# Graph network kernel, scatter stage: GpSimd's pause in mid-group waits for three scatters instead of four

## What is computed

```
x_i, x_j = x[dst_or_src of each edge], edge_attr: 64 numbers of each edge
out_i = act(concat(x_i, edge_attr) @ W)            # 4 heads of 64
out_j = act(concat(x_j, edge_attr) @ W)
alpha = act((concat(out_i, out_j) * att).sum(-1))  # one number of each edge and head
alpha = act(batch_norm(alpha))
alpha = segment_softmax(alpha, i)                  # over the edges with the same i = src
x = layernorm(x + segment_sum(out_j * alpha, i).mean(heads) + bias)
h = gcn_conv(gcn_conv(x, src, dst, W1, b1), src, dst, W2, b2)
x = layernorm(x + relu(h))
```

## Time and profile before

| | |
|---|---|
| median of 3 runs | 7369.46 us |
| profiled execution, its own time | 7374.29 us |
| its span in the profile | 7372.1 us |
| from the first scatter of the scatter stage to the last | 534.65 to 3270.51 us |
| scatters in it | 1616, in 202 groups |
| busy share over the whole span | TensorE 69%, VectorE 72%, ScalarE 55%, GpSimd 27% |
| mean granted TensorE clock over the span | 0.861 of full speed |

### The profile page before, as it was taken

How to read it: one execution, slowest core, us unless ns; L and a number is a source line. 1 busy time by engine, 2 the same in 40 slices (tenths; PEclk the granted TensorE clock), 3 DMA queues, 4 the chain that set the end, 5 groups by cost and what they waited for, 6 DMA issues and landing times. The chain is left out here.

```text
span 7372.1 us, 162457 instructions
## 1 busy us (share of the span) xinstructions
PE 5061.6 (69%) x33039; PEld 3158.5 (43%) x33040; DVE 5308.0 (72%) x27929; ACT 4071.5 (55%) x10690; POOL 2017.3 (27%) x2671
## 2 busy tenths in 40 slices
PE   1226766666666766637777777777724999995877
PEld 0113444344344443424444444444413555554877
DVE  5626666666666666629999999999987888887122
ACT  0015555455555555537777777777735889884000
POOL 0035555555655555541111111111100000000000
PEclk8557778778888778869999999999967999997978
DMA  4565555555555555555555555555514878773956
GB/s 33 219 226 166 178 165 177 169 165 178 170 177 168 171 174 164 172 175 144 144 145 145 144 146 144 144 145 145 144 34 121 214 213 222 213 214 103 381 225 258
DMA packets 905819, 1259.82 MB, mean 171 GB/s; under 512 B 267668, under 2 KB 774531, under 8 KB 884180
## 3 DMA queue, kind: packets, MB, share of 16 engines
q1 hardware_dynamic: 783812, 843.53, 41.2%
q0 software_dynamic: 88656, 333.99, 12.1%
q10 hardware_dynamic: 33216, 80.75, 3.2%
HBM read 832.07 MB, written 425.87 MB: 171 GB/s over the span
## 5 line engine op out<-in xcount | busy, mean ns | idle before, releaser
L840 POOL DMA_INDIRECT rows<-rowS,idx x1616 | 1605.0, 993 | 1151.7 <-DMA rows<-rowS,idx 605.1
L1530 DVE CUSTOM_DVE_ANT_1 junk<-bufh,attb 128x128 bf16<-128x128 f32 x7296 | 1693.7, 292 | 3.7 <-ACT bufh L1570 3.7
L1096 PE MATMUL psa<-one_c,one_s 128*128 128x392 bf16 x2352 | 651.4, 395 | 763.7 <-issue 322.7
L2219 PE MATMUL psm<-msg,onem 128*128 128x260 f32 x3648 | 1011.5, 402 | 135.1 <-issue 50.8
L989 ACT ACTIVATE lgS<-preS 128x1024 f32<-128x1024 f32 x404 | 412.7, 1021 | 893.0 <-remote 638.3
L2219 PEld LDWEIGHTS psm<-msg,onem 128*128 128x128 f32 x3648 | 619.1, 189 | 527.0 <-issue 473.0
L1502 POOL COPY eaC<-bufh 128x128 f32<-128x128 f32 x912 | 322.0, 353 | 1793.9 <-DMA bufh<-rows 1789.1
L923 DVE TENSOR_SCALAR one_c<-ioc,code 128x392 bf16<-128x392 f16 x2352 | 779.1, 331 | 18.3 <-DVE code L915 3.7
L1566 ACT ACTIVATE lg<-pre 128x512 f32<-128x512 f32 x912 | 544.9, 598 | 423.4 <-PE pre L1609 423.3
L2186 DVE TENSOR_TENSOR msg<-oj,alpha 128x512 f32<-128x512 f32 x912 | 631.1, 692 | 185.7 <-issue 96.7
L915 DVE TENSOR_SCALAR code<-pairS,codes 128x3 f32<-128x3 f32 x784 | 201.4, 257 | 782.2 <-remote 531.8
(11 more groups left out here) (275 smaller groups left out, 8107.7 us busy)
## 6 DMA issues: line engine op xcount, KB each, us to landing
bufh<-rows SPq DMA_DIRECT2D x912, 322.0 KB, 3.0
oj<-rows SPq DMA_DIRECT2D x912, 256.0 KB
adj<-adj SPq DMA_DIRECT2D x98, 1568.0 KB, 8.4
adj<-cnts ACTq DMA_DIRECT2D x49, 1568.0 KB
eaS<-in_edge_attr_dram SPq DMA_DIRECT2D x201, 256.0 KB
low<-dlow SPq DMA_DIRECT2D x202, 252.0 KB
rows<-fill POOLq DMA_DIRECT2D x20, 1610.0 KB
rows<-fill POOLq DMA_DIRECT2D x100, 322.0 KB
```

The lines of the kernel that those rows point to most:

```text
L840: eng.indirect_dma_start(out=m["rows"][h], out_offset=bass.IndirectOffsetOnAxis(ap=idx[s][:, k:k + 1], axis=0), in_=rows[s][:, k, :], in_o ...
L1096: mm = eng.matmul(psa[r][:, 0:z.GC], one_s[r][:, k, :], one_c[r][:, k, :], start=(k == 0), stop=(k == GT - 1))
L1530: ins = eng.tensor_tensor_reduce(junk[q][:, k * H + h, :, :], buf[j][:, k, :, h * D:(h + 1) * D], attb[:, :, h, :], 1.0, 0.0, ALU.mult, AL ...
L2219: mm = eng.matmul(psm[j][:, 0:C + H], one[q][:, k, :], msg[q][:, k, :], start=(k == 0), stop=(k == UT - 1))
```

## The change

A scatter k with k < FIRST = K // 2 - 1 = 3 now signals a semaphore of its own, `early[s]`. The other five (k = 3 to 7) still signal `sent[s]`. The pause waits for `early[s]`, that is for the scatters k = 0, 1 and 2 of this group, and no longer for k = 3. The three waits for `sent` elsewhere count five scatters in a group instead of eight. The instructions and their order are the same on every engine.

```diff
+    FIRST = K // 2 - 1
...
+        early = [sem(ctx, f"early{s}") for s in range(NR_BUF)]
         sent = [sem(ctx, f"sent{s}") for s in range(NR_BUF)]
...
                         eng.indirect_dma_start(
                             out=m["rows"][h], out_offset=bass.IndirectOffsetOnAxis(ap=idx[s][:, k:k + 1], axis=0),
-                            in_=rows[s][:, k, :], in_offset=None).then_inc(sent[s], 16)
+                            in_=rows[s][:, k, :], in_offset=None).then_inc(early[s] if k < FIRST else sent[s], 16)
                     if part == 0:
-                        eng.wait_ge(sent[s], b * 16 * K + 16 * K // 2)
+                        eng.wait_ge(early[s], (b + 1) * 16 * FIRST)
...
-                eng.wait_ge(sent[s], (NG + NR_BUF - 1 - s) // NR_BUF * 16 * K)
+                eng.wait_ge(sent[s], (NG + NR_BUF - 1 - s) // NR_BUF * 16 * (K - FIRST))
...
-                wait(eng, sent[s], b * 16 * K)
+                wait(eng, sent[s], b * 16 * (K - FIRST))
                 eng.tensor_copy(rows[s][:, :, LO], m["nlo"][:, span(t * K, K)])
...
-                wait(eng, sent[s], b * 16 * K)
+                wait(eng, sent[s], b * 16 * (K - FIRST))
                 eng.wait_ge(ea_in[s % 2], ea_landed(b, s))
```

## The result

The changed kernel takes 7507.5 us, the median of four runs (7499.45 to 7530.64), against 7368.3 us for the kernel before. The ratio is 1.0191, with a 95% interval of 1.0161 to 1.0221. That is 139 us slower, on the side of rival C and outside the predicted range. The profiled execution has a span of 7528.5 us.

The account below looks back on a forecast made before the run. The scatter stage was taken as bound by waits, with GpSimd like a server behind a queue. Gains of 9 us (last groups) and 74 us (the other 195) made 83 us, so 7369.5 - 83 = 7286 us, range 7150 to 7500.

Parts of the forecast that it names:

- rival C: Scatter stage: the shorter pause no longer lets held-up signals through, so engines stay held; 155 us slower, 7525 us; 37%.
- The pause: GpSimd's mid-group idle time falls from 2.4 to 1.1 us, 1.27 us less in each of 202 groups, 257 us at most.
- Rival D: Landings of k = 2 and k = 3 bunch, so the pause stays as long; 7369 us; 18% together with no change.
- The semaphore and the counts at nothing: The new semaphore and wait counts add or move no instruction, so they cost nothing.
- Scatters and VectorE at nothing: Scatters overlapping a little more with VectorE cost 0; doubling today's collision loss would cost 48 us more.
- The comparison with 3.1 us: A skill text gives 3.1 us for a transfer blocked by VectorE; no scatter took over 1.41 us, so the trace disagrees.
- A faster GpSimd lives in this regime: In the first 195 groups GpSimd soon catches up with ScalarE; pace 13.18 us instead of 13.56, 74 us gained.
- The last seven groups: From group 195 on GpSimd alone works off its queue, so each group gains 1.27 us, 9 us in all.
- point of decision: Rival C hangs on a needed quiet time between 0.30 and 1.4 us; at under 1.1 us it is dead.
- One of its signs: Under rival C, remote waits of ScalarE's Exp and VectorE's `code` grow beyond 638 and 532 us, ending at a group's start.
- The reading of the earlier trace: In two groups ScalarE's Exp and VectorE's `code` come loose inside GpSimd's pause, 1.38 to 1.90 us after k = 3.
- Rival A: The whole pause time is gained because the other engines follow GpSimd's rhythm; 257 us, 7112 us; 20% with anything between.

Follow-up runs that it names:

- e1: Changed kernel with FIRST = K // 2, so the pause waits for all four scatters on the new semaphore: 7368.2 us, ratio 0.9993 to the kernel before.
- e3: Changed kernel plus a 1.3 us GpSimd memset behind the early wait, lengthening the time without scatters: 7363.4 us, ratio 0.9992 to the kernel before.
- e4: Changed kernel with the pause moved behind k = 2, still waiting for k = 0, 1 and 2: 7401.1 us, ratio 1.0036 to the kernel before.
- h_after: The changed kernel itself, run again on a chip where the kernel before takes 7517.0 us: 7373.4 us, ratio 0.9805.
- j_first_two: Changed kernel with two scatters on the early semaphore instead of three, pause still behind k = 3; before at 7512.4 us: 6770.6 us, ratio 0.9014.
- f_m20: Kernel before with the mid-group landing wait replaced by a GpSimd memset of about 2.0 us; before at 7511.2 us: 7116.4 us, ratio 0.9472.
- g_no_pause_again: Kernel before with the mid-group landing wait removed and nothing in its place; before at 7514.9 us: 6753.3 us, ratio 0.8988.
- g_tiny: Kernel before with the mid-group landing wait replaced by a GpSimd memset of 8 numbers a partition; before at 7514.9 us: 6755.4 us.

## Why the prediction was wrong

- *The pause.* Right in kind: the landing of k = 2 ends it, under 1.2 us after k = 3 in 82 of 202 groups and 1.27 in the median, about as the earlier trace rows less 1.27 gave (1.1). The landing waits fell to 223 us, further than the 350 forecast. Rival D falls.
- *The semaphore and the counts at nothing.* Right (e1, 0.9993).
- *Scatters and VectorE at nothing.* Right: 985 ns in the mean, 993 before, and none over 1444 ns. The comparison with 3.1 us proves less than it says, since no instruction of VectorE in that stage lasts over 0.63 us, and none could keep a scatter waiting for 3.1 us by itself.
- *"A faster GpSimd lives in this regime … I take 13.18 as the pace with the shorter pause."* This step failed. It priced the changed kernel by a stretch of before, in which each group still had its pause of 2.4 us. The other engines' pace was held constant, while the change touches just what sets it. With the shorter pause the first 195 groups take 2811.9 us, 14.42 each, not 13.18. The term of 74 us gained came as 167 us lost. GpSimd's waits for the Ln went to 472 us, not to about 250. The last seven groups gained 6 us for the 9 forecast.
- *Rival C* named the mechanism, and its size came out close: 14.40 us a group from the earlier trace rows, 155 us slower forecast, 139 measured. That it came so close is partly luck, since it took every group for starved, while 107 of 201 groups began after more than 1 us of idle time (14 before). Its point of decision was right too, since 1.1 us is mostly too short on this chip. One of its signs was wrong: the remote waits of Exp and `code` fell. The held-up time went to earlier waits, the counts and `ranks`. The part on their ends was half right: they left the pause behind k = 3, but only 130 of 393 moved to a group's start.
- *The reading of the earlier trace rows.* For the Exp it holds. For VectorE it doesn't: the row puts `code`'s wait down to a load of the pairs and not to a remote signal, and in the next group `code` starts at 2028.96, when k = 4 has just begun, and again behind such a load. The 531.8 us of remote waits are real but were not looked at.
- *The weights.* The 37% for C rested on two groups and on "may simply be the latency of that event". Counted over the stage, the same trace has 292 of 367 such waits ending in the pauses, which are 24% of it. That is no chance. It could not tell a latency from a needed quiet time, though. That took the runs: a shorter pause loses (7507.5), the same early landings with a longer quiet time don't (e3, 7363.4), and the ends follow the pause when it is moved (e4).
- *Rival A* was not wrong in general. On chips without the hold the change gains 144 us of A's 257, and no pause at all gains 762 (7514.9 to 6753.3 us).

## What to carry to other kernels

A wait that looks like pure loss on a saturated engine may be the window in which other engines' signals and instructions get through. Before shortening it, count over the whole stage where the others' unexplained waits end: if most end at a fixed time inside it, price the change by the stretches in which the window was missed. When a dummy instruction fills the window, look at what it does to the other engines, as the memset did to VectorE here. And for a change whose value hangs on such a thing, one chip is not enough: the changed kernel stands at 1.019 to before here and at 0.981 there.

## What the hardware showed that I had not expected

- Chips differ in kind. On some (two at least, before at 7368 to 7427 us) indirect scatters of GpSimd at 0.30 us from each other hold up TensorE's instructions and its signals to ScalarE and VectorE. A gap of 0.9 to 1.5 us ended 18 of 91 open waits, every gap of 1.8 us or more ended all of them (129 in the changed kernel). On four others (before at 7511 to 7533 us) there is not one such wait. Which setting or part makes the difference, no run here shows.
- The hold reaches TensorE's own issue: tiny matmuls that take 0.03 us apart (29 in 0.87 us) come at steps of 0.7 or 1.4 us while scatters run (226 such steps in the changed kernel, 60 before). Waits for "issue" before this line are 196.2 us in the changed kernel on kind one, and none in the same kernel on kind two (h_after).
- The kind on which before is faster is the slower one for most other versions: without a pause 7558 against 6753 us. Of the versions run on both kinds (the changed kernel, no pause, the 2.0 us memset) none beats before on both. On kind two the kernel without a pause is the best (ratio 0.8988). On kind one nothing was measurably faster than before.
- A landing wait on kind two goes from 0.44 us to 3.1 us when it asks for one scatter later (j_first_two and h_after). The cause is open.
- A memset on GpSimd holds VectorE. With one of 2.0 us in each group, 473 of VectorE's instructions took over 1 us, up to 2.86 us, and its busy time was 2195 us where it is 1771 without one (f_m20 and g_no_pause_again). With a memset of 8 numbers there was not one (g_tiny).
